# Moving the base product ahead in each turn, routing's side work off VectorE, and half-size last expert tiles

## The chip, the cores and the metric

One core of a Trainium2 chip runs the whole kernel. Its engines are TensorE (PE; its weight loads are listed as PEld), VectorE (DVE), ScalarE (ACT), GpSimd (POOL) and SyncE (SP, which only issues DMAs here). The metric is the device time of one execution in microseconds.

## The reference

The input x is 8 sequences of 512 rows of 128 numbers. After a layernorm (`xn`), the output is `x + attn(xn) + ffn(xn)`.

```python
def attn(x):                      # its x is xn; w is a vector of 127 biases by distance
    xn = (x - mean) / sqrt(var + EPS) * ln_w + ln_b
    u, v, base = split(silu(xn @ uv_w.T + uv_b), [256, 256, 128])
    q, k = rope(base * gamma[0] + beta[0]), rope(base * gamma[1] + beta[1])
    kernel = square(relu(q @ k.T / sqrt(128) + w[clipped distance]))
    return (u * (kernel @ v)) @ o_w.T + o_b + x

def ffn(x):                       # 4096 tokens, 8 experts, hidden width 512
    probs = sigmoid(x @ W_router); the two best of 8, weights p / (p1 + p2 + 1e-6)
    out = sq_relu(x @ W_sh_up) @ W_sh_down
    for e in the two experts: out += weight[e] * (sq_relu(x @ W_up[e]) @ W_down[e])
```

`rope` makes of the two halves x1, x2 of the 128 numbers `x1 cos - x2 sin` and `x2 cos + x1 sin`.

## The kernel before

The five engines run five programs written out by hand; they meet only at semaphores, and each engine works strictly in the order in which its program is written. Features lie on the 128 partitions, the 512 rows of a sequence along the columns.

**Turns.** A turn does one sequence: attention and the shared expert. Turns 0 to 6 come first, then the expert loop, then turn 7. `x1` is the once normalised sequence (for the shared expert and the router), `x2` the twice normalised one (for attention). Products that need precision are done as three matmuls in the type float32r on operands split in a high and a low part (`product`, lines L1021 to L1023, labelled `f32` in the profile's rows): ScalarE writes the high part, VectorE subtracts it from the operand for the low part. The others are plain f32 (`L1115` kernel times v, `L1101` shared down, `L1121` output, `L1284` expert down). A TensorE turn is, in order: the gates u0 and u1; two of the four shared up products sh0, sh1; the value products v0, v1 (12 matmuls of 256 columns); the scores qk0 to qk3, with the previous sequence's output product in their middle; sh2, sh3; two shared down products; the transposes `fin` of the previous sequence's output; kernel times v in four parts, between whose parts the next sequence is prepared (transposes of x2, the products `base` and `bsw`, transposes of x1); the last shared down products. `bsw` is the product for `base` with its two halves of features exchanged, so that the rotation needs no exchange. All of these go through a ring of four PSUM banks (`RING`): a product may start once the result four places before it has been read.

ScalarE turns `base` and `bsw` into two SiLU tiles and four scaled tiles `base_qk` (q and k, each plain and exchanged); VectorE multiplies by cos and sin (`rotate_base`) and adds (`rotate_sum`); ScalarE makes `qk_hi` from that, then the SiLU of u0 and u1, behind which the value products stand in the ring.

**Routing** is laid over turns 0 to 3. In turns 0 and 1 TensorE transposes each sequence's x1 once more (`rt`) and makes the router's products, eight columns each (`L1049`). At the end of turn 1 VectorE picks the two best experts of each token (`routing_first`, `routing_second`, semaphore `chosen_made`). In turn 2 TensorE counts (`routing_counted`), and VectorE makes the weights, running sums of the counts, each expert's number of tiles and the slot of each token (`routing_weights`, `routing_counts`, `routing_tiles`, `routing_slots`). With the slots (`slots_made`) GpSimd scatters the 4096 tokens in 64 indirect DMAs to `slots_in` in HBM, at most two in flight. In turn 3 VectorE makes the owners of the tiles (`routing_owners`); from it SyncE loads the expert weights.

**The expert loop** runs 39 tiles of 256 slots (`PAIR` = 2 halves of 128), enough for any distribution of the tokens. Step s transposes tile s, makes the up products of tile s - 1 (12 matmuls of 256 columns) and the down products of tile s - 2 (for each half four plain f32 matmuls of 128 columns); GpSimd sends the rows of tile s - 3 to `results`. Before the first step TensorE waits for `mixed` (turn 6's output added to x on VectorE) and for the slot load, which SyncE issues once all tokens have landed. The first 36 steps are in a loop unrolled by four, the rest is written out. Behind the last step VectorE does `rotate_base(7)`, TensorE turn 7; SyncE fetches the experts' rows (`fetch`) as soon as the last are home; VectorE adds them to x (`combine`), and SyncE stores.

## Time and profile before

| | us |
|---|---|
| three runs, median | 392.57 |
| their lowest and highest | 390.35, 453.52 |
| the profiled execution | 391.36 |
| its span | 389.5 |

| engine | busy, us | share of the span |
|---|---|---|
| TensorE | 351.0 | 90% |
| VectorE | 275.1 | 71% |
| ScalarE | 228.4 | 59% |
| GpSimd | 171.0 | 44% |

The span is what the trace shows from the first to the last record; the execution's own time is 1.9 us more. A busy share is a mean over stages with different limits, so the stages have to be looked at one by one. The mean granted clock of TensorE was 0.98 of full speed. In the timeline a row has the start, the busy time, engine, line, operation, `written<-read`, a count, and in brackets how long the engine stood idle before and what released it.

### The profile page before, as it was taken

What the parts mean: (1) busy time and instruction counts of PE and PEld (TensorE: products, weight loads), DVE (VectorE), ACT (ScalarE), POOL (GpSimd) and SP (SyncE); (2) the same over time, 40 slices, a digit from 0 to 9 for tenths busy, and PEclk for the clock granted to TensorE, in tenths of its full rate; (3) what the DMA queues carried; (4) which work ended last, traced back from release to release, by engine and by line L of the source; (5) the groups of instructions that cost most, each with busy time, mean ns of one, the idle gap of its engine ahead of it and who ended that gap; (6) DMA issues with size and microseconds to landing.
All of it is one profiled execution on the core that took longest, in us unless ns stands there. A gap on an engine that the chain in (4) does not pass through costs nothing.

```text
span 389.5 us, 6982 instructions
## 1 busy us (share of the span) xinstructions
PE 351.0 (90%) x1984; PEld 269.4 (69%) x1985; DVE 275.1 (71%) x646; ACT 228.4 (59%) x418; POOL 171.0 (44%) x161
## 2 busy tenths in 40 slices
PE   1779979989989999999996999999999999999791
PEld 1565658556556565756644989899899999998540
DVE  3879465789997774947643776777777777776876
ACT  0774996474653756646363767676676666772610
POOL 3004600000076377677760265666656566667000
PEclk9989999999999999999996999999999999999997
DMA  6999300000014811111112354544444446521795
GB/s 159 307 276 257 70 0 2 0 0 3 0 42 126 268 48 48 37 55 48 50 48 68 98 158 120 160 129 143 156 130 148 137 135 156 140 84 49 202 301 151
DMA packets 56836, 43.88 MB, mean 113 GB/s; under 512 B 6673, under 2 KB 49041, under 8 KB 56817
## 3 DMA queue, kind: packets, MB, share of 16 engines
q1 hardware_dynamic: 50304, 32.71, 32.6%
q0 software_dynamic: 4544, 9.38, 6.7%
q10 hardware_dynamic: 1968, 1.55, 1.3%
q8 instruction: 9, 0.15, 0.2%
q14 instruction: 11, 0.08, 0.1%
HBM read 26.36 MB, written 17.26 MB: 112 GB/s over the span
## 4 chain that ended last, share of the span: by engine, by line
PE 53%; DVE 16%; DMA 10%; ACT 10%; issue 6%; POOL 2%; ACTq 1%; DVEq 1%; SPq 0%
PE bank L1284 11%; DMA slot_x<-slots_in 9%; PE bank L1021 8%; PE bank L1115 8%; PE bank L1023 7%; PE bank L1022 7%; ACT base_qk L484 3%; PE bank L1101 3%; PE bank L1121 3%; PE bank L1261 2%; DVE work L762 2%; DVE work L756 2%; PE bank L1078 1%; ACT work L446 1%; ACT work L497 1%
## 5 line engine op out<-in xcount | busy, mean ns | idle before, releaser
L1008 POOL DMA_INDIRECT results<-work,dest x78 | 90.4, 1159 | 67.5 <-issue 22.4
L993 POOL DMA_INDIRECT slots_in<-work,slot_i x64 | 65.4, 1022 | 87.8 <-issue 62.6
L1284 PE MATMUL bank<-wdn,work 128*128 x624 | 76.1, 275 | 0.1
L1284 PEld LDWEIGHTS bank<-wdn,work 128*128 128x128 f32 x624 | 73.0, 192 | 0.3 <-issue 0.3
L1115 PE MATMUL bank<-kern,v 128*128 128x512 f32 x128 | 58.7, 592 | 0.0
L593 ACT ACTIVATE work<-bank 128x512 f32<-128x512 f32 x78 | 46.6, 600 | 6.5 <-PE bank L1023 3.9
L1021 PE MATMUL bank<-sx_lo,w_hi 128*128 128x256 f32 x156 | 48.3, 310 | 1.4 <-DVE w_lo L900 1.4
L1022 PE MATMUL bank<-sx_hi,w_lo 128*128 128x256 f32 x156 | 44.6, 286 | 0.0
L1023 PE MATMUL bank<-sx_hi,w_hi 128*128 128x256 f32 x156 | 44.5, 285 | 0.0
L584 ACT CAST sx_hi<-bank 128x256 fp32r<-128x256 f32 x39 | 14.5, 373 | 43.9 <-PE bank L1261 43.9
L906 DVE TENSOR_TENSOR work<-work 128x512 f32<-128x512 f32 x39 | 27.1, 694 | 18.7 <-ACT work L593 18.7
L1115 PEld LDWEIGHTS bank<-kern,v 128*128 128x128 f32 x128 | 22.7, 190 | 20.6 <-issue 20.6
L503 ACT ACTIVATE work<-bank 128x512 f32<-128x512 f32 x32 | 18.4, 600 | 27.0 <-PE bank L1101 26.0
L916 DVE TENSOR_SCALAR work<-bank,row_sum 128x128 f32<-128x128 f32 x78 | 27.2, 348 | 8.9 <-PE bank L1284 7.7
L1021 PEld LDWEIGHTS bank<-sx_lo,w_hi 128*128 128x128 f32 x156 | 30.1, 193 | 3.4 <-DVE sx_lo L897 1.8
L1022 PEld LDWEIGHTS bank<-sx_hi,w_lo 128*128 128x128 f32 x156 | 30.2, 194 | 0.0
L1101 PE MATMUL bank<-work,shdn 128*128 128x512 f32 x64 | 30.1, 593 | 0.0
L1023 PEld LDWEIGHTS bank<-sx_hi,w_hi 128*128 128x128 f32 x156 | 30.1, 193 | 0.0
L900 DVE TENSOR_TENSOR w_lo<-region,w_hi 128x512 fp32r<-128x512 f32 x39 | 26.8, 687 | 1.0
L586 ACT CAST w_hi<-region 128x512 fp32r<-128x512 f32 x39 | 24.3, 624 | 0.0
L597 ACT ACTIVATE work<-work 128x512 f32<-128x512 f32 x39 | 24.3, 622 | 0.0
L785 DVE SCALAR_TENSOR_TENSOR kern<-kern 128x512 f32<-128x512 f32 x32 | 22.2, 694 | 1.1
(163 smaller groups left out, 671.2 us busy)
## 6 DMA issues: line engine op xcount, KB each, us to landing
region<-in_L_ffn_W_up SPq DMA_DIRECT2D x39, 256.0 KB, 2.8
slots_in<-zeros SPq DMA_DIRECT2D x1, 5148.0 KB, 24.7
slot_x<-slots_in SPq DMA_DIRECT2D x39, 132.0 KB
region<-results SPq DMA_DIRECT2D x12, 256.0 KB, 5.0
wdn<-in_L_ffn_W_down SPq DMA_DIRECT2D x4, 512.0 KB, 6.3
out<-x_all SPq DMA_DIRECT2D x8, 256.0 KB, 2.3
results<-work,dest POOLq DMA_INDIRECT x78, 3.4
x_all<-in_L_attn_x SPq DMA_DIRECT2D x2, 512.0 KB, 7.6
```

The lines of the kernel that those rows point to most:

```text
L593: act.activation(hid_t[:, h, 2 * m:2 * m + 2, :].rearrange("p c s -> p (c s)"), P_UP[h][m][:, :], ACT.Relu)\
L900: dve.tensor_tensor(w_lo[:, j % 2, :], w_raw[:, j % 4, :], w_hi[:, j % 2, :].bitcast(F32), ALU.subtract).then_inc(w_lo_made, 1)
L906: dve.tensor_tensor(kept, kept, kept, ALU.mult).then_inc(hid_b_made, 1)
L916: dve.tensor_scalar(slot_y[:, k, :], P_Y[half][:, 0:D], times, None, ALU.mult).then_inc(y_made, 1)
L993: pool.indirect_dma_start(slots_in, bass.IndirectOffsetOnAxis(slot_i[:, k, t:t + 1], 0), xs1[:, t, at], None, element_offset=k * 2).then_i ...
L1008: pool.indirect_dma_start(results, bass.IndirectOffsetOnAxis(dest[:, at:at + 1], 0), slot_y[:, k, :], None).then_inc(returned[k], 16)
L1021: pe.matmul(dst, w_hi, m_lo, start=start, stop=False)
L1022: pe.matmul(dst, w_lo, m_hi, start=False, stop=False)
L1023: return pe.matmul(dst, w_hi, m_hi, start=False, stop=stop)
L1101: pe.matmul(P_OUT[:, :], shdn[:, c, :], sh[:, c % 2, :], start=(c == 0), stop=False).then_inc(shdn_done, 1)
L1115: last = pe.matmul(P_AV[e][:, :], v[:, j, e * P:(e + 1) * P], kern[:, j, :], start=(j == 0), stop=(j == TB - 1))
L1284: last = pe.matmul(P_Y[half][:, 0:D], hid_t[:, h, c, half * P:(half + 1) * P], wdn[:, of, c, :].rearrange("p a d -> p (a d)"), start=(c == ...
```

## The change

**Base chain.** The exchanged product `bsw` is gone. ScalarE makes one SiLU tile and two `base_qk` tiles. VectorE exchanges the halves as it multiplies by sin: two operations on 64 partitions each, which read one half and write the other. The next sequence's x2 transposes and base product move ahead of the shared down products and of kernel times v, and with them the work of ScalarE and VectorE on them. Sequence 7's rotation comes before the expert loop.

**x1.** The separate transposes of x1 are gone; the router's transposed copy is kept for all eight sequences (`route_xt`), and the split of x1 reads it.

**Routing.** The weights (sum, reciprocal, product) are GpSimd's; the copies of the counts and the second norm of sequences 2 and 3 are ScalarE's. The clearing of `sums` moves to turn 0. The split of x2 comes ahead of the routing steps.

**Tiles.** An expert's 128-slot halves are counted: its pairs go to full tiles, a last odd half to an own tile behind all full ones. There are still 39 tiles; the first 35 have 256 slots, the last four 128.

```diff
+FULL = (TOPK * NT + NE - 1) // PAIR
+SLOT_TILES = PAIR * FULL + TILES - FULL
...
-            RING += [("fin", b - 1)] if 0 < b < LAST else []
+            RING += [("x2", b + 1), ("fin", b - 1), ("base", b + 1)] if 0 < b < LAST else []
...
-            elif b < LAST:
-                RING += [("x2", b + 1), ("base", b + 1), ("bsw", b + 1), ("x1", b + 1)]
...
+                act.activation(silu_b[:, :], of_ring("base", b), ACT.Silu, bias=uvbias[:, 2:3]).then_inc(silu_b_made, 1)
+                act.wait_ge(silu_b_made, START + b + 1)
+                for k in range(2):
+                    act.activation(base_qk[:, k, :], silu_b[:, :], ACT.Identity, bias=bet[:, k:k + 1], scale=gam[:, k:k + 1])\
+                       .then_inc(base_made, 1)
...
+                if 0 < b < LAST:
+                    second_rows_hi(b + 1)
                 shared_relu(b, 2)
                 shared_relu(b, 3)
+                if 0 < b < LAST:
+                    base_silu(b + 1)
...
             def routing_tiles():
-                link(route_chain, dve.tensor_scalar(tiles_i[:, :], run[:, 15 + NT, :], float(PAIR * P - 1), None, ALU.add))
-                link(route_chain, dve.tensor_scalar(tiles_n[:, :], tiles_i[:, :], 8, None, ALU.logical_shift_right))
-                link(route_chain, dve.tensor_copy(ends[:, 0, 4:], tiles_n[:, :]))
-                for n in range(3):
+                pairs, odd = slice(0, NE), slice(NE, 2 * NE)
+                link(route_chain, dve.tensor_scalar(tiles_i[:, :], run[:, 15 + NT, :], float(P - 1), None, ALU.add))
+                link(route_chain, dve.tensor_scalar(tiles_i[:, :], tiles_i[:, :], 7, None, ALU.logical_shift_right))
+                link(route_chain, dve.tensor_scalar(parts_n[:, pairs], tiles_i[:, :], 1, None, ALU.logical_shift_right))
+                link(route_chain, dve.scalar_tensor_tensor(parts_n[:, odd], parts_n[:, pairs], -2.0, tiles_i[:, :], ALU.mult, ALU.add))
+                link(route_chain, dve.tensor_copy(ends[:, 0, 8:], parts_n[:, :]))
+                dve.tensor_scalar(in_pairs[:, :], ends[:, 0, 8:8 + NE], float(PAIR * P), None, ALU.mult)
+                for n in range(4):
...
             def routing_slots():
                 link(route_chain, dve.tensor_tensor(place, run[:, 15:15 + NT, :], place, ALU.add))
+                link(route_chain, dve.tensor_tensor(others, place, of_expert(in_pairs), ALU.is_ge))
+                link(route_chain, dve.tensor_tensor(others, others, of_expert(to_tail), ALU.mult))
+                link(route_chain, dve.tensor_tensor(place, place, of_expert(starts), ALU.add))
+                link(route_chain, dve.tensor_tensor(place, place, others, ALU.add))
...
+                for to, of in ((slice(0, HALF), slice(HALF, S)), (slice(HALF, S), slice(0, HALF))):
+                    dve.tensor_tensor(rot2[to], base_qk[of], cos_sin[of, 1:2, :].broadcast_to([HALF, 2, T]), ALU.mult)\
+                       .then_inc(rot2_made, 1)
...
+            pool.wait_ge(chosen_made, 1)
+            pool.tensor_tensor(denom[:, :], weight[:, 0, :], weight[:, 1, :], ALU.add).then_inc(weight_chain, 1)
...
+            pool.tensor_tensor(denom[:, :], denom[:, :], minus_one[:, :], ALU.pow).then_inc(weight_chain, 1)
...
+                    width = n.parts() * P
                     for c in range(HC):
-                        of = slice(c * P, (c + 1) * P)
-                        last = product(P_UP[h][c // 2][:, c % 2 * PAIR * P:(c % 2 + 1) * PAIR * P], w_hi[:, h, of], w_lo[:, h, of],
-                                       sx_hi[:, h, :], sx_lo[:, h, :])
+                        of, to = slice(c * P, (c + 1) * P), c % 2 * PAIR * P
+                        last = product(P_UP[h][c // 2][:, to:to + width], w_hi[:, h, of], w_lo[:, h, of],
+                                       sx_hi[:, h, 0:width], sx_lo[:, h, 0:width])
```

On VectorE in turn 2, before, the running sums (L716) stand ahead of the split of x2 (L671), the mix (L799, L802) and the tile counts (L722 on):

```order
L785 SCALAR_TENSOR_TENSOR kern<-kern 128x512
L712 COPY wdn<-bank 128x256
L713 COPY wdn<-bank 128x256
L716 TENSOR_TENSOR wdn<-wdn 128x256 x5
L671 TENSOR_TENSOR x_lo<-bank,x_hi 128x512
L799 TENSOR_TENSOR x_all<-x_all,work 128x512
L802 TENSOR_TENSOR x_all<-bank,x_all 128x512
L722 TENSOR_SCALAR tiles_i<-wdn 128x8
```

After, on VectorE, from the tile counts of turn 2 to the rotation (the split of x1 is L713, the slots L770 to L778, the exchange L799):

```order
L764 TENSOR_TENSOR to_tail<-to_tail,starts 128x8
L713 TENSOR_TENSOR x_lo<-region,x_hi 128x512
L770 TENSOR_TENSOR wdn<-wdn 128x256
L771 TENSOR_TENSOR wdn<-wdn,in_pairs 128x256
L772 TENSOR_TENSOR wdn<-wdn,to_tail 128x256
L773 TENSOR_TENSOR wdn<-wdn,starts 128x256
L774 TENSOR_TENSOR wdn<-wdn 128x256
L778 CAST slot_i<-slot_f 128x64
L796 TENSOR_TENSOR work<-base_qk,cos_sin 128x1024
L799 TENSOR_TENSOR work<-base_qk,cos_sin 64x1024 x2
```

The split of x2 now stands ahead of the sums, the split of x1 ahead of the slots, and the exchange takes two operations where one stood.

On TensorE in a middle turn, before, the next sequence's transposes (L1078) and base products stand between the parts of kernel times v (L1115), behind the shared down products (L1101) and `fin` (L1128):

```order
L1101 MATMUL bank<-work,shdn 128x512 x2
L1128 MATMUL bank<-cst,work 128x128 x4
L1115 MATMUL bank<-kern,v 128x512 x2
L1078 MATMUL bank<-cst,xs 128x128 x4
L1115 MATMUL bank<-kern,v 128x512 x2
...
L1078 MATMUL bank<-cst,work 128x128 x4
L1115 MATMUL bank<-kern,v 128x512 x4
L1101 MATMUL bank<-work,shdn 128x512 x2
```

After, at the same place (transposes L1134, shared down L1157, `fin` L1184, kernel times v L1171):

```order
L1134 MATMUL bank<-cst,xs 128x128 x4
L1157 MATMUL bank<-work,shdn 128x512 x2
L1184 MATMUL bank<-cst,work 128x128 x4
L1079 MATMUL bank<-x_lo,uvw_hi 128x512
L1080 MATMUL bank<-x_hi,uvw_lo 128x512
L1081 MATMUL bank<-x_hi,uvw_hi 128x512
L1171 MATMUL bank<-kern,v 128x512 x8
L1157 MATMUL bank<-work,shdn 128x512 x2
```

The transposes of x2 have moved ahead of the shared down products, one base product stands before kernel times v, and the transposes of x1 are gone.

## Rows read from the trace of the kernel before

**Rows 1.** Windows: busy of PE, PEld, DVE, ACT, POOL; granted clock; DMA.

```profile
24.80:26.90 2.10, 0.06 (x2) 0.05 (x1) 1.32 (x2) 1.56 (x3) 0.00 (x0) 1.00 1.24 276
26.90:30.30 3.40, 3.40 (x8) 2.75 (x9) 3.37 (x12) 2.27 (x4) 0.00 (x0) 0.50 1.26 253
141.50:165.00 23.50, 23.33 (x90) 14.52 (x89) 15.95 (x25) 13.71 (x22) 16.97 (x16) 1.00 0.15 47
328.70:357.10 28.40, 28.30 (x241) 27.42 (x239) 19.70 (x59) 17.92 (x35) 19.21 (x18) 1.00 0.36 103
```

**Rows 2.** Timeline: slot numbers, first scatter, first slot load, loop's start.

```profile
106.20 0.20 DVE L737 CAST slot_i<-slot_f 128x64 int32<-128x64 f32 x1
107.35 1.22 POOL L993 DMA_INDIRECT slots_in<-work,slot_i  x1 [57.75 <-issue]
204.34 7.50 SPq L364 DMA_DIRECT2D slot_x<-slots_in  x3
206.68 0.69 DVE L802 TENSOR_TENSOR x_all<-bank,x_all 128x512 f32<-128x512 f32 x1 [2.31 <-PE bank L1128]
208.28 1.11 PE L1261 MATMUL bank<-cst,slot_x 128*128 128x128 f32 x4 [1.65 <-DVE x_all L802]
```

**Rows 3.** Timeline: PE, the next sequence's base products and transposes, turn 4.

```profile
150.45 0.40 PE L1023 MATMUL bank<-x_hi,uvw_hi 128*128 128x512 f32 x1
150.69 0.60 PE L1078 MATMUL bank<-cst,work 128*128 128x128 f32 x4
151.13 3.60 PE L1115 MATMUL bank<-kern,v 128*128 128x512 f32 x8
```

**Rows 4.** Timeline: PE, first value product of turns 2 and 3.

```profile
86.56 0.39 PE L1021 MATMUL bank<-uvw_lo,x_hi 128*128 128x256 f32 x1 [1.39 <-ACT work L497]
112.36 0.39 PE L1021 MATMUL bank<-uvw_lo,x_hi 128*128 128x256 f32 x1 [1.39 <-ACT work L497]
```

**Rows 5.** Timeline: ACT, end of turn 0; PE, shared down products of turn 1.

```profile
45.25 1.26 ACT L479 ACTIVATE work<-bank,uvbias 128x512 f32<-128x512 f32 x2
46.40 1.52 ACT L484 ACTIVATE base_qk<-work,bet,gam 128x512 f32<-128x512 f32 x2
55.27 1.06 ACT L517 CAST qk_hi<-work 128x1024 fp32r<-128x1024 f32 x1
69.22 1.88 PE L1101 MATMUL bank<-work,shdn 128*128 128x512 f32 x4
```

**Rows 6.** Timeline: DVE, turns 1 and 2.

```profile
79.15 0.42 DVE L698 TENSOR_TENSOR wdn<-wdn 128x256 f32<-128x256 f32 x1
81.62 1.23 DVE L756 TENSOR_TENSOR work<-base_qk,cos_sin 128x1024 f32<-128x1024 f32 x1 [0.18 <-ACT base_qk L484]
97.73 2.26 DVE L716 TENSOR_TENSOR wdn<-wdn 128x256 f32<-128x256 f32 x5
100.03 0.69 DVE L671 TENSOR_TENSOR x_lo<-bank,x_hi 128x512 fp32r<-128x512 f32 x1
102.64 0.57 DVE L727 TENSOR_TENSOR ends<-ends 128x8 f32<-128x8 f32 x3
```

**Rows 7.** Timeline: PE, one expert tile (`x16`: two records a product).

```profile
276.21 0.28 PE L1023 MATMUL bank<-sx_hi,w_hi 128*128 128x256 f32 x1
276.33 1.95 PE L1284 MATMUL bank<-wdn,work 128*128 x16
278.11 0.38 PE L1261 MATMUL bank<-cst,slot_x 128*128 128x128 f32 x2
```

**Rows 8.** Chain of waits: 8-column products (two records each); a slot load.

```profile
65.72 0.79 PE bank L1049 x8
215.93 2.12 DMA slot_x<-slots_in
```

**Rows 9.** Timeline: start of the last turn.

```profile
357.58 0.50 PE L1021 MATMUL bank<-x_lo,uvw_hi 128*128 128x512 f32 x1 [0.45 <-DVE work L916]
362.84 0.38 PE L1021 MATMUL bank<-uvw_lo,x_hi 128*128 128x256 f32 x1 [2.24 <-ACT work L497]
```

312 lines of the change are left out of this document (166 added, 146 removed).

## The prediction

> **What bounds the kernel now.** I read the windows first, to see which engine is full where. In the middle turns TensorE works 23.33 of 23.50 us, and in the last stretch of the expert loop 28.30 of 28.40 [rows 1]; VectorE, ScalarE and GpSimd have room in both. So an edit pays in such a stretch only if it takes work off TensorE. The timeline then shows a second resource, which no share of busy time gives away: the scatter of the tokens. GpSimd issues 64 row scatters one behind the other, the first at 107.35, right after the slot numbers (106.20 + 0.20), and the first load of slots, which waits for all 64 to land, is issued at 204.34 [rows 2]. That is 97.9 us of pipeline, fixed by the first scatter. TensorE reaches the loop at 208.28, having waited for VectorE's last sum at 207.37 and then issued for 0.9 us [rows 2]. A slot load lands 2.1 us after its issue [rows 8], so data were there at about 206.5, and the scatter lies only some 2 us behind TensorE. What TensorE saves in the turns is worth no more than that, plus whatever the slot numbers move. The last stretch, from 357.58 on, is TensorE's turn 7 and then VectorE's sums; it begins with a wait of 2.24 us for the rotation [rows 9].
>
> **The turns.** Per sequence TensorE loses the product for `bsw` (three matmuls, 0.23 apart: 0.69 us) and the four transposes for `x1` (150.69 to 151.13: 0.44) [rows 3]: 1.13 us, of a turn of 23.5. The base product also moves from the middle of the value products to before them, so ScalarE and VectorE have 6.9 us more for the rotation; the short wait before the value products (23.50 - 23.33, and as much hidden in modelled ends) should go. I take 22.0 us a turn where nothing else binds. VectorE pays for it: the half swap is now two operations on 64 partitions instead of one on 128. Time on this engine goes with the columns of a partition (256 columns 0.42, 512 0.69, 1024 1.23 [rows 6]), so each half costs 1.23 and not 0.6, a pitch of 1.13 with the overlap: +1.13 a sequence, in cover except in turns 1 and 2, where routing fills VectorE.
> By the Trainium skill ("VectorE: DVE Perf Modes", Two Vector instructions with no wait between them) an operation whose input or output starts in another quadrant than the last one's is held until all earlier ones have finished. The trace has no such pair; by the rule each half would lose the overlap of about 0.1 us and the slot numbers below would come 0.2 to 0.3 us later. The sum below is made without it.
>
> **The slot numbers, step by step.**
> Turn 0 ends on ScalarE, which runs without a gap from 45.25 to 56.3. It loses one SiLU of two (half of 1.15) and two of the four `base_qk` (1.41) [rows 5], 2.0 us; the shorter start (no `x1` transposes, one product less) gives 0 to 0.5 more. I take 2.2: turn 1's shared up products, done at 69.2 before [rows 5], are done at 67.0.
> Turn 1: the transposes of x2 come right behind it (0.44), then ScalarE's copy and the split (0.6 + 0.7 [rows 6]) to 68.75; now `routing_first` (five operations of 0.46 pitch, 2.3) to 71.1, the mix of two 512-wide operations to 72.5, `routing_second` (seven of 0.46, 3.2) to 75.7. It ended at 79.57 before [rows 6], so chosen is 3.9 earlier. Then three rotation operations (3.4), `x1_lo` (0.6) and the sum (1.2): queries ready at 81.0; ScalarE's copy and SiLU, 1.9, and the first value product at 82.9 instead of 86.56 [rows 4]: 3.6 earlier.
> Turn 2: value products 1.44, counts 0.8, scores at 85.1; four scores, the output product and two shared products (5.9) bring TensorE to 91.0, with VectorE no longer in the way, since the routing weights, the second norm and two copies are gone from it. x2 split at 92.7, the counts' five additions (2.3 [rows 6]) to 95.0, the mix to 96.4. Then what the change adds: 13 linked operations of 0.2 (the three of 102.64 take 0.6 [rows 6]) and two unlinked, 2.85 instead of 1.4; the x1 split, 0.6; nine operations of 256 columns (five take 2.26 [rows 6]) where there were six, and the cast, 4.3. Slot numbers at 104.2 instead of 106.4: **2.2 us earlier**. The routing weights on GpSimd have from 75.7 to 104 to themselves: GpSimd idled 57.75 us before its first scatter [rows 2], so any price below some 28 us is hidden; ScalarE's copies and second norm lie in its idle time.
>
> **The price in turn 3.** Rotation comes behind the slot numbers: 104.2 + 3.4 + 1.2 = 108.8, then 1.9 on ScalarE: first value product of turn 3 at 110.9, before at 112.36 [rows 4]. TensorE will have been done with turn 3's shared up products at 105.7 (91.0, its remaining work of turn 2, 11.9, and 2.8), so it stands idle some 5 us. In the trace 2.1 idle us, from 24.8, were followed by 3.4 us at a granted clock of 0.50, the lower level of 1.2 GHz [rows 1]; the same again costs 1.7 us. TensorE's arrival: 110.9 + 1.7 + 3 turns of 22.0 = 178.6, plus the rest of turn 6 up to the loop (before from 112.36 + 3 x 23.5 = 182.9 to 208.28, 25.4; less 1.13) = 202.9. The scatter gives 204.34 - 2.2 + 2.2 = 204.4, which is later. So the loop starts at 204.4 instead of 208.28: **-3.9 us**, and of the 8 to 10 us that TensorE's own work shrinks half is lost waiting for the scatter.
>
> **The last turn.** Queries and keys of sequence 7 are ready before the loop. Today TensorE would reach the value products at 357.58 + 12 x 0.23 = 360.35 and starts them at 362.84 [rows 9]: **-2.5 us**. The next late thing is `fetch`, 16 loads behind the last returns; the returns come some 2 us sooner behind TensorE too, since the last tiles send one half each, so I leave it hidden; if not, it costs up to 1.
>
> **The tail tiles.** A full tile is two transposes (0.24), 12 products of the f32r type over 256 columns, 0.12 apart (1.43), and eight plain f32 products of 128 columns in 1.78, 0.22 each [rows 7]: 3.45. A half tile has one transpose (0.12), four such down products (0.89) and 12 up products over 128 columns, whose price no row shows. From below: half of 256 columns, 0.06 each. From above: the plain f32 product of the same 128 columns and the same four bytes, 0.22 [rows 7]. In between lies a floor by the weights: a product over only 8 columns still takes 0.10 a record [rows 8]. At 0.22 a half tile is 0.12 + 2.67 + 0.89 = 3.7 and four are 0.9 dearer than four full ones; TensorE's last waits in the loop (0.1 a tile) go under, so **+0.6 us** (0 to 0.9). At 0.10 a half tile is 2.2 and the four give 5.0; at 0.06 they would give 6.9, but VectorE still splits the whole 512 columns of weights for every tile, and I stop at 6. I take 0.22: the row with the same width and the same bytes, while 256 and 512 columns (0.12, 0.23) show only that the cheap rate holds from 256 up.
> By the Trainium skill ("TensorE: Matmul & The Clock Gate", LDWEIGHTS) a weight load takes columns / 1.2 ns, 107 ns for 128, and the 8-column rows at 0.10 agree. By that alone the up part is 12 x 0.107 = 1.28, and the time would be the first rival's.
>
> **Sum.** The profiled execution took 391.36: a span of 389.5 and 1.9 around it, and the runs shown have their median at 392.57, so the sum is 1.2 under what a median might show. 391.36 - 3.9 - 2.5 + 0.6 = 385.5, a gain of 1.5%. A measurement of this kernel tells about 2% from nothing.
>
> **Rivals.**
> A. Narrow products at the weight load's price or less (0.06 to 0.10). For it: the type ran at one column a clock at both widths shown. Against: no row under 256. 391.36 - 3.9 - 2.5 - 5.0 = 380.0, faster by 2.9%. Chance 0.34.
> B. The slot numbers come 2 us or more before 104.2, because VectorE overlaps its small operations or turn 0 shrinks by more. Then TensorE's arrival, 202.9, binds, and with tails as forecast the time is 384.0, 1.9% faster. For it: each step above was taken at its full pitch. Against: nine waits in a row, each only as early as its predecessor. Chance 0.10.
> C. The scatter slows down, and the kernel with it. Its pitch is 97.9 / 64 = 1.5 us; it now lies beside a denser TensorE and VectorE, and its rows share the DMA engines with the w_down and w_up loads. Each 0.1 us of pitch costs 6.4 us. From 1.6 the gain is gone, and at 1.7 it is 385.5 + 12.8 = 398.3, slower than before. Against: its pitch is steady across turns of very different load, and GpSimd touches none of the moved work. Chance 0.04.
> The forecast itself has 0.52.
>
> **How the numbers follow.** Own range of the forecast: 383.5 to 387.5 (slot numbers 1 us either way, `fetch` 1 us). Over all cases 378.8 to 388.0: the lower end takes in the tail's 5.0 and its 6, and C is left out. Faster by over 2% means under 383.5: all of A, a fifth of B and some of the forecast, 0.38; slower by over 2%, 0.03; within, 0.59.
>
> **What the next profile would show.** First scatter near 105.1 and slot load near 202; an idle time of about 5 us on TensorE before turn 3's value products with the clock at 0.50 behind it; middle turns of 22.0; TensorE waiting for the slot load, not for VectorE, at the loop's start; in the tail up products 0.22 apart; no wait of 2.24 in the last turn. I am wrong if the up products are 0.10 or less apart, or if the slot numbers do not move by 1 to 3 us.

## The result, and the profile after

The changed kernel takes 390.2 us (median of 20 runs, 387.0 to 395.1), the kernel before 392.95 (20 runs). The ratio, taken like all ratios below from the fast runs of both kernels, is 0.993 [0.990, 0.995] (in brackets its 95% interval): a gain of 0.7%, no difference at 2%. Forecast was 385.5, the range ended at 388.0. The profiled execution took 395.13, a span of 393.3, which is 4.9 over its median, so its stages are checked below against the traces of other kernels that share them.

**Turns, timeline and windows** (columns as in [rows 1]). First the slot numbers, the first scatter, the issue of the first slot loads, turn 6's last sum and the loop's first transposes:

```profile
106.07 0.20 DVE L778 CAST slot_i<-slot_f 128x64 int32<-128x64 f32 x1
107.33 1.23 POOL L1051 DMA_INDIRECT slots_in<-work,slot_i  x1 [19.79 <-issue]
206.79 0.90 SPq L374 DMA_DIRECT2D slot_x<-slots_in  x2
204.42 0.69 DVE L845 TENSOR_TENSOR x_all<-bank,x_all 128x512 f32<-128x512 f32 x1 [1.12 <-PE bank L1184]
209.10 0.69 PE L1313 MATMUL bank<-cst,slot_x 128*128 128x128 f32 x2 [4.71 <-DMA slot_x<-slots_in]
```

Against [rows 2] the slot numbers moved by 0.1 us and not by 2.2, so the scatter did not move either; TensorE was ready earlier and waited 4.71 us. A middle turn, the stretch behind turn 3's wait, the body of the expert loop, and the last tiles:

```profile
141.50:163.50 22.00, 22.00 (x83) 13.78 (x82) 17.27 (x26) 12.15 (x20) 16.51 (x16) 1.00 0.15 49
110.00:118.00 8.00, 4.80 (x17) 4.38 (x18) 5.50 (x7) 5.03 (x9) 6.36 (x6) 0.63 0.13 42
215.00:325.00 110.00, 105.32 (x862) 100.69 (x861) 78.90 (x231) 73.37 (x147) 64.18 (x55) 0.99 0.47 136
352.60:366.00 13.40, 12.30 (x58) 11.27 (x59) 3.28 (x10) 3.92 (x10) 3.83 (x4) 0.62 0.06 24
```

A middle turn is full at 22 us. The body of the loop is not: 862 records of TensorE in 110 us, and the same stretch of the kernel before had 884 (below). The stretch with the last tiles ran at a mean granted clock of 0.62.

TensorE in turns 2 and 3 (first value product, then two value products and one product of the scores), and VectorE at the end of turn 2, against [rows 4] and [rows 6]:

```profile
84.71 0.39 PE L1079 MATMUL bank<-uvw_lo,x_hi 128*128 128x256 f32 x1 [1.36 <-ACT work L520]
113.20 0.58 PE L1079 MATMUL bank<-uvw_lo,x_hi 128*128 128x256 f32 x1 [5.42 <-ACT work L520]
113.58 0.41 PE L1080 MATMUL bank<-uvw_hi,x_lo 128*128 128x256 f32 x1
113.79 0.41 PE L1081 MATMUL bank<-uvw_hi,x_hi 128*128 128x256 f32 x1
116.35 0.63 PE L1080 MATMUL bank<-qk_hi,qk_lo 128*128 128x512 f32 x1
```
```profile
98.53 0.16 DVE L750 TENSOR_SCALAR tiles_i<-wdn 128x8 int32<-128x8 f32 x1
101.34 0.69 DVE L713 TENSOR_TENSOR x_lo<-region,x_hi 128x512 fp32r<-128x512 f32 x1
...
106.18 1.22 DVE L796 TENSOR_TENSOR work<-base_qk,cos_sin 128x1024 f32<-128x1024 f32 x1
107.43 2.47 DVE L799 TENSOR_TENSOR work<-base_qk,cos_sin 64x1024 f32<-64x1024 f32 x2
110.00 1.23 DVE L805 TENSOR_TENSOR work<-work 128x1024 f32<-128x1024 f32 x1
```

In turn 3 products stand 0.21 us apart where 0.12 is usual: the engine had idled 5.42 us. The half-partition operations take 1.24 each with no overlap.

**The tail, timeline of TensorE.** L1313 are transposes (of tiles 33, 34, 35 and 38, counted from 0; half tiles from 342.14 on), L1337 down products, the others up products:

```profile
332.95 0.38 PE L1313 MATMUL bank<-cst,slot_x 128*128 128x128 f32 x2
338.65 0.44 PE L1313 MATMUL bank<-cst,slot_x 128*128 128x128 f32 x2 [2.10 <-DMA slot_x<-slots_in]
342.14 0.27 PE L1313 MATMUL bank<-cst,slot_x 128*128 128x128 f32 x1
348.86 0.28 PE L1080 MATMUL bank<-sx_hi,w_lo 128*128 128x128 f32 x1
348.98 0.27 PE L1081 MATMUL bank<-sx_hi,w_hi 128*128 128x128 f32 x1
349.09 0.28 PE L1079 MATMUL bank<-sx_lo,w_hi 128*128 128x128 f32 x1
352.62 0.33 PE L1313 MATMUL bank<-cst,slot_x 128*128 128x128 f32 x1 [1.42 <-DMA slot_x<-slots_in]
356.18 0.41 PE L1079 MATMUL bank<-sx_lo,w_hi 128*128 128x128 f32 x1
356.39 0.41 PE L1080 MATMUL bank<-sx_hi,w_lo 128*128 128x128 f32 x1
363.26 0.80 PE L1079 MATMUL bank<-x_lo,uvw_hi 128*128 128x512 f32 x1 [0.44 <-DVE work L961]
366.72 0.28 PE L1079 MATMUL bank<-uvw_lo,x_hi 128*128 128x256 f32 x1
```

Narrow up products are 0.11 apart. But two waits for slot loads stand here, and behind the second one the products are 0.21 apart: the granted clock was 0.50, the lower level of 1.2 GHz, from 354.3 to 364.6. In the last turn the value products (366.72) follow without the wait of [rows 9].

**One step of the loop** shows what those waits are. Timeline of VectorE, SyncE and TensorE, transposes of tiles 21 and 22 (L961 weights the down products' result, L974 makes the destinations, L374 is the slot load):

```profile
288.07 0.38 PE L1313 MATMUL bank<-cst,slot_x 128*128 128x128 f32 x2
288.27 0.35 DVE L961 TENSOR_SCALAR work<-bank,row_sum 128x128 f32<-128x128 f32 x1 [0.20 <-PE bank L1337]
289.21 0.23 DVE L974 TENSOR_TENSOR dest<-row_sum,spare_row 128x2 int32<-128x2 f32 x1 [0.21 <-DVE spare_row L971]
289.62 0.37 SPq L374 DMA_DIRECT2D slot_x<-slots_in  x1
292.11 0.44 PE L1313 MATMUL bank<-cst,slot_x 128*128 128x128 f32 x2 [0.44 <-DMA slot_x<-slots_in]
```

There are two slot buffers. With s = 20 in these rows: the load for tile s + 2 waits until VectorE has taken the destinations of tile s out of the buffer, and VectorE does that last in its step, behind the two weightings of tile s - 2 (`step` on VectorE). So it is issued 1.5 us after the transposes of tile s + 1 have begun, and 2.5 us after its issue TensorE begins to transpose what it brought, 4.04 us behind the last transposes. For a tile TensorE needs 3.45 us, so it waits.

A table by stages, all from the transposes' and first gate products' starts in the traces (start of the loop; to tile 3; from there to tile 35 and per tile; to turn 7's u0; to the end of the span). The kernels are those of the experiments below. The traces of after and full_same are of executions 4.9 and 3.8 us over the kernel's median; the others are within 1.6 of theirs.

| kernel | loop starts | to tile 3 | 32 tiles (each) | rest of loop | last turn |
|---|---|---|---|---|---|
| before | 208.28 | 9.8 | 119.5 (3.73) | 20.0 | 31.9 |
| after | 209.10 | 10.4 | 122.6 (3.83) | 21.1 | 30.0 |
| full_same | 207.83 | 11.3 | 121.3 (3.79) | 23.8 | 29.4 |
| full_short | 205.13 | 10.9 | 119.1 (3.72) | 20.0 | 29.5 |
| flight4 | 206.09 | 10.1 | 122.0 (3.81) | 17.5 | 29.5 |
| before_slots4_e | 209.58 | 8.8 | 111.1 (3.47) | 20.8 | 33.4 |
| slots4 | 207.75 | 9.2 | 110.5 (3.45) | 16.2 | 29.4 |
| slots4_full_e | 206.35 | 9.8 | 110.5 (3.45) | 19.7 | 29.4 |
| best | 202.79 | 9.5 | 110.5 (3.45) | 16.2 | 29.5 |

### The profile page after: what moved, and what is told of

Same layout as the page of the kernel before. It is cut to its first block, busy times and chain, and to the rows that moved or that the text cites. A ratio compares the mean times of both kernels' runs of the same rounds, so it can differ in the third digit from the quotient of the medians.

```text
span 393.3 us, 6680 instructions
## 1 busy us (share of the span) xinstructions
PE 345.5 (88%) x1891; PEld 266.7 (68%) x1892; DVE 282.8 (72%) x647; ACT 214.9 (55%) x404; POOL 179.2 (46%) x164
## 4 chain that ended last, share of the span: by engine, by line
PE 34%; DMA 31%; DVE 15%; issue 7%; ACT 6%; POOL 5%; DVEq 0%; SPq 0%; POOLq 0%; ACTq 0%
DMA slots_in<-work,slot_i 19%; PE bank L1337 11%; DMA slot_x<-slots_in 11%; PE bank L1079 6%; PE bank L1081 5%; PE bank L1080 5%; POOL slots_in L1051 3%; PE bank L1313 2%; ACT work L456 2%; PE bank L1171 2%; POOL inv L990 1%; DVE work L799 1%; DMA x_all<-in_L_attn_x 1%; PE bank L1134 1%; DVE wdn L667 1%
## 5 line engine op out<-in xcount | busy, mean ns | idle before, releaser
L1337 PE MATMUL bank<-wdn,work 128*128 x592 | 75.3, 281 | 0.6 <-DVE work L961 0.6
L1337 PEld LDWEIGHTS bank<-wdn,work 128*128 128x128 f32 x592 | 71.8, 197 | 0.9 <-issue 0.9
L1171 PE MATMUL bank<-kern,v 128*128 128x512 f32 x128 | 56.7, 592 | 0.0
L1079 PE MATMUL bank<-sx_lo,w_hi 128*128 128x256 f32 (+1 forms) x156 | 49.0, 314 | 1.4 <-DVE w_lo L945 1.4
L631 ACT ACTIVATE work<-bank 128x512 f32<-128x512 f32 (+1 forms) x78 | 45.0, 577 | 9.4 <-PE bank L1081 6.7
L1081 PE MATMUL bank<-sx_hi,w_hi 128*128 128x256 f32 (+1 forms) x156 | 45.5, 292 | 0.0
L1080 PE MATMUL bank<-sx_hi,w_lo 128*128 128x256 f32 (+1 forms) x156 | 45.4, 291 | 0.0
L1171 PEld LDWEIGHTS bank<-kern,v 128*128 128x128 f32 x128 | 24.1, 190 | 26.8 <-issue 26.3
L620 ACT CAST sx_hi<-bank 128x256 fp32r<-128x256 f32 (+1 forms) x39 | 14.1, 362 | 50.5 <-PE bank L1313 50.5
L951 DVE TENSOR_TENSOR work<-work 128x512 f32<-128x512 f32 (+1 forms) x39 | 25.9, 665 | 19.0 <-ACT work L631 18.8
L961 DVE TENSOR_SCALAR work<-bank,row_sum 128x128 f32<-128x128 f32 x74 | 25.8, 348 | 11.7 <-PE bank L1337 11.5
L1157 PE MATMUL bank<-work,shdn 128*128 128x512 f32 x64 | 30.2, 594 | 0.0
L1313 PE MATMUL bank<-cst,slot_x 128*128 128x128 f32 x74 | 16.2, 301 | 13.0 <-DMA slot_x<-slots_in 12.8
L540 ACT CAST qk_hi<-work 128x1024 fp32r<-128x1024 f32 x8 | 8.4, 1046 | 33.9 <-DVE work L805 33.9
L526 ACT ACTIVATE work<-bank 128x512 f32<-128x512 f32 x32 | 18.8, 598 | 12.5 <-PE bank L1157 11.1
L825 DVE SCALAR_TENSOR_TENSOR kern<-bank,bias_t 128x512 f32<-128x512 f32 x32 | 21.9, 685 | 4.2 <-PE bank L1081 4.2
```

The costliest lines, as they stand in the source:

```text
L631: act.activation(hid_t[:, h, 2 * m:2 * m + 2, 0:width], made, ACT.Relu).then_inc(relu_done, 1)
L951: dve.tensor_tensor(kept, kept, kept, ALU.mult).then_inc(hid_b_made, 1)
L961: dve.tensor_scalar(slot_y[:, k, :], P_Y[half][:, 0:D], times, None, ALU.mult).then_inc(y_made, 1)
L1079: pe.matmul(dst, w_hi, m_lo, start=start, stop=False)
L1080: pe.matmul(dst, w_lo, m_hi, start=False, stop=False)
L1081: return pe.matmul(dst, w_hi, m_hi, start=False, stop=stop)
```

## The experiments

Two theories stood at first: S, that the scatter binds the loop's start, so that what the turns save is lost there, and T, that in the tail a slot load's round trip is longer than a half tile. After experiment 2 a third took T's place: L, that this round trip paces the whole loop. Ratios are to the kernel before.

**1. Four scatters in flight (flight4): 387.19 us, 0.986 [0.981, 0.992].**

```diff
-        IN_FLIGHT = TOPK
+        IN_FLIGHT = 2 * TOPK
```

> The changed kernel with four scatters of tokens in flight instead of two; nothing else differs. In its trace the 64 scatters take 97 us, of which GpSimd's own issues are 69.2 and waits for landed rows 23.7, and TensorE waits 4.71 us for the first slot load before the loop and then works 6 us at the lower clock. Theory S (the scatter binds the loop's start, so what the turns save is lost there): the pitch falls from 1.52 to 1.3 or less, the load of slots is issued at 190 or before, the wait of 4.71 goes, the loop starts at about 205.5 (behind turn 6's last sum) instead of 209.1 with a shorter stretch at the lower clock: 384 to 386.5 us, a ratio of 0.978 to 0.984 against the kernel before. Rival (GpSimd's issues set the pitch, not the landings): pitch 1.45 or more and the time stays at 390, ratio 0.993.

The loop starts behind turn 6's sum, not behind the load:

```profile
198.27 11.12 SPq L374 DMA_DIRECT2D slot_x<-slots_in  x3
```
```profile
206.09 0.65 PE L1313 MATMUL bank<-cst,slot_x 128*128 128x128 f32 x4 [1.65 <-DVE x_all L845]
```

The load is issued 8.5 us earlier, a pitch of (198.27 - 107.42) / 64 = 1.42 and not the 1.3 expected: GpSimd's own issues fill 69 of these 91 us. TensorE's arrival, 206.1, takes over after 3.0 us. So the scatter did bind the loop's start in the changed kernel, but removing that gave only 3.0 us (0.7%; the two intervals still touch), and the time missed the expected 386.5: the loop remained 149.7 us long.

**2. Four slot buffers (slots4): 375.28 us, 0.957 [0.953, 0.961].**

```diff
-        slot_x = sb("slot_x", [P, 2, 2, ROW_W])
+        slot_x = sb("slot_x", [P, 4, 2, ROW_W])
...
-                    sp.wait_ge(sx_turned, i * UNROLL + (j + 1))
                     sp.wait_ge(dest_made, i * (PAIR * UNROLL) + PAIR * (j + 1))
-                    load_slots(j, ds(i * (PAIR * UNROLL) + PAIR * (j + 2), PAIR))
+                    load_slots(j, ds(i * (PAIR * UNROLL) + PAIR * (j + 4), PAIR))
```

> The changed kernel with four buffers for the loaded slots instead of two, so a tile's load may be issued four steps ahead (SyncE no longer waits for the transposes by name; the destinations come behind them). Theory T (in the tail the round trip of a slot load, transposes, destination, load of 2.8 us, over two short steps is longer than the steps; TensorE waits 1.42 and 0.64 us and falls to the lower clock for 9 us; another wait of 2.10 hits a full tile): waits for slot loads go from the whole loop but for its start, the tail's four tiles run 0.11 us a product at the higher clock, 3.5 to 5.5 us less: ratio 0.980 to 0.985. Rival (the waits are those of the loads' own queue, which is busy, or of VectorE): the waits stay at other loads, and the ratio is 0.99 or more.

Both theories fell short: the gain is not 3.5 to 5.5 us but 15. The round trip paced every tile, not the tail alone. Body of the loop, then TensorE's waits for slot loads from the loop's start to turn 7 (total, times, longest), first of this kernel:

```profile
215.00:325.00 110.00, 110.00 (x958) 109.60 (x958) 85.61 (x257) 79.84 (x161) 72.44 (x62) 1.00 0.50 151
```
```profile
PE bank L1312 <- DMA slot_x<-slots_in: 3.6, 2, 3.4
```

and of the changed kernel with two buffers:

```profile
PE bank L1313 <- DMA slot_x<-slots_in: 12.8, 16, 4.7
```

In 110 us TensorE now has 958 records instead of 862. The waits listed fell by 9.2 us, the loop by 154.2 - 135.8 = 18.4, and against flight4's trace, which is not of a long execution, by 13.8. The modelled ends of the matmuls cover a part of each wait: in the changed kernel the transposes stand by turns some 3.6 and 3.9 to 4.0 us apart, the list has 0.2 to 0.4 of the longer step and nothing of the shorter, and the distance from one tile's transposes to the next tells it whole.

**3. The tail undone (full_same: 391.77 us, 0.995 [0.991, 0.998]) and with it its routing (full_short: 387.74, 0.988 [0.984, 0.993]).** In the first, whose edit is shown, all 39 tiles are full but the long routing stays; in the second `routing_tiles`, `routing_slots` and `routing_owners` are those of the kernel before.

```diff
-FULL = (TOPK * NT + NE - 1) // PAIR
+FULL = TILES
...
-                link(route_chain, dve.tensor_scalar(tiles_i[:, :], run[:, 15 + NT, :], float(P - 1), None, ALU.add))
-                link(route_chain, dve.tensor_scalar(tiles_i[:, :], tiles_i[:, :], 7, None, ALU.logical_shift_right))
-                link(route_chain, dve.tensor_scalar(parts_n[:, pairs], tiles_i[:, :], 1, None, ALU.logical_shift_right))
-                link(route_chain, dve.scalar_tensor_tensor(parts_n[:, odd], parts_n[:, pairs], -2.0, tiles_i[:, :], ALU.mult, ALU.add))
+                link(route_chain, dve.tensor_scalar(tiles_i[:, :], run[:, 15 + NT, :], float(PAIR * P - 1), None, ALU.add))
+                link(route_chain, dve.tensor_scalar(tiles_i[:, :], tiles_i[:, :], 8, None, ALU.logical_shift_right))
+                link(route_chain, dve.tensor_scalar(parts_n[:, pairs], tiles_i[:, :], 0, None, ALU.logical_shift_right))
+                link(route_chain, dve.scalar_tensor_tensor(parts_n[:, odd], parts_n[:, pairs], -1.0, tiles_i[:, :], ALU.mult, ALU.add))
```

> The changed kernel with 39 full tiles: the tail is undone, while routing keeps its added operations (an expert's odd half gets a full tile; the factor for odd halves is zero). Theory T (the tail's cheaper products are eaten by slot load waits and the lower clock): within 1 us of the changed kernel, ratio 0.990 to 0.998. Rival N (narrow products at 0.11 us really give 4 x 1.1 us, and the loss is only upstream, at the scatter and the clock): 3.5 to 4.5 us slower than the changed kernel, ratio 1.001 to 1.005.

> The changed kernel with the tail undone and the routing of tiles, slots and owners as in the kernel before: only the turns and routing's side work are changed. Against the run with 39 full tiles and the long routing it shows what the added operations on VectorE cost: the slot numbers should come 1.4 + 1.3 = 2.8 us before 106.3, and by theory S the whole scatter, the first slot load and the loop start 2.8 us earlier too, so 2.5 to 3 us less than that run (ratio lower by 0.007). Rival (TensorE binds the loop's start, the scatter does not): less than 1 us between the two.

Half tiles gave 0.2% in the changed kernel (0.993 against 0.995, whose intervals overlap), as theory T said, and not rival N's 1%. The long routing cost 0.6% by the ratios, 2.5 us (4.0 by the medians), though these intervals too overlap; the start of the loop moved by 2.7 (207.83 to 205.13), close to the 3.0 us by which the slot numbers moved (106.04 to 102.99):

```profile
102.99 0.20 DVE L765 CAST slot_i<-slot_f 128x64 int32<-128x64 f32 x1
104.25 1.23 POOL L1036 DMA_INDIRECT slots_in<-work,slot_i  x1 [17.48 <-issue]
```
```profile
205.13 1.23 PE L1298 MATMUL bank<-cst,slot_x 128*128 128x128 f32 x4 [4.82 <-DMA slot_x<-slots_in]
```

So the tail part of the change as a whole lost, by 0.993 with it to 0.988 without (390.2 and 387.7 us); the two intervals, [0.990, 0.995] and [0.984, 0.993], overlap, so the time alone does not prove it, while the 3 us at the slot numbers and at the loop's start are in the traces.

**4. Was the kernel before paced too (before_slots4)?** The edit of experiment 2 in the kernel before.

> The kernel before with four buffers for the loaded slots instead of two; nothing of the change. Theory L (the slot load's round trip, not TensorE, paces the expert loop in the kernel before too: its transposes stand 3.74 us apart over 38 tiles, where the run with four buffers has 3.44): the loop falls from 149.3 to about 138.5, so 381 to 383 us, ratio 0.970 to 0.975, and the change is then worth 6 to 8 us between the two kernels with four buffers. Rival (TensorE paces the loop before, as its busy share of the last stretch said; only the changed kernel's loop suffers): ratio 0.99 or more.

This experiment was one of ten (before_slots4, slots4_full, slots4_flight4 and slots4_filler, each once more as _b, and before_slots4_c and slots4_full_c) that fell on three chips (6, 8 and 15 in the record) on which the kernel before itself took 441 to 443 us by its median: in the turns, while the scatter ran, ScalarE and VectorE stood still for 10 to 40 us at a time, as in this row of ScalarE in slots4_flight4:

```profile
197.30 1.26 ACT L519 ACTIVATE work<-bank,uvbias 128x512 f32<-128x512 f32 x2 [39.38 <-remote]
```

Its repeats:

> The kernel before with four slot buffers once more, since on the chip of the first try engines stood still for 10 to 40 us in the turns, in every kernel. In that trace the transposes of the loop already stood 3.44 us apart where nothing else was late. Theory L: ratio 0.970 to 0.975. Rival (TensorE paced the loop before): 0.99 or more.

> One look at the kernel before with four slot buffers. Theory L: the loop's transposes 3.44 to 3.5 us apart instead of 3.74, loop from first transposes to the last turn's first product 138 to 140 us instead of 149.3, and a time of 381 to 383 where the kernel before takes 392.5. Rival (TensorE paced the loop before): 3.7 apart, 389 or more.

The first gave 436.7 us, a ratio of 0.992 [0.987, 0.998], which is the rival's number; the others took 439.6 beside 442.5, and 445.9 beside 440.9. With halts of this length in the turns I take nothing from these times (there the kernel with four scatters in flight was 20 us behind its neighbours, which no theory here explains). A single run on a chip without the halts (before_slots4_d) took 384.06 beside 392.97, with the transposes 3.43 to 3.6 apart:

> One look at the kernel before with four slot buffers, on another occasion. Theory L: loop from first transposes to the last turn's first product 138 to 140 us instead of 149.3, 381 to 383 where the kernel before takes 392.5. Rival: transposes 3.7 apart, 389 or more.

And six runs there:

> The kernel before with four slot buffers, timed in rounds (the look at it took 384.06 where the kernel before took 392.97). Theory L: ratio 0.973 to 0.980. The change is then worth, between the two kernels with four buffers, 0.9568 over that ratio, 1.7 to 2.4%. Rival (the look was a lucky one): 0.985 or more.

Measured: 384.24 us, 0.978 [0.974, 0.982], as theory L said. The body of the loop, of the kernel before and with four buffers:

```profile
215.00:325.00 110.00, 106.03 (x884) 101.83 (x883) 80.94 (x238) 74.40 (x149) 66.02 (x57) 1.00 0.48 139
```
```profile
215.00:325.00 110.00, 110.00 (x951) 109.10 (x950) 85.15 (x254) 80.30 (x162) 70.65 (x61) 1.00 0.49 149
```

The kernel before was paced by the slot load, at 3.73 us a tile where TensorE needs 3.47. With four buffers in both, the change is worth 0.957 / 0.978 = 0.978, 9 us. By the table, of the 10.6 us between the two spans the loop's start has 1.8, the rest of the loop 4.6 and the last turn 4.0. Not all of that is half tiles and rotation: this run's turn 7 begins behind a wait of 1.53 us, where the kernel before waited 0.45, and its value products, behind the same wait for the rotation as before (2.23), ran at a granted clock of 0.50 from 355.4 to 358.8, where the kernel before ran at full rate; that is 1.1 and about 1.5 us.

**5. Half tiles once loads do not pace (slots4_full_e).** Experiments 2 and 3 (first) together.

> The changed kernel with four slot buffers and with 39 full tiles, routing's added operations kept: what the half tiles are worth once loads do not pace the loop. Theory L: TensorE sets the tail's pace, a half tile costs 12 x 0.11 + 8 x 0.11 + 0.12 = 2.3 to 2.4 us instead of 3.44, so the run is 4 to 4.5 us slower than the one with four buffers and half tiles: 379.5, ratio 0.966 to 0.969. Rival (the tail stays bound by VectorE, ScalarE or the weights' loads, so half tiles give little): within 1.5 us of it, ratio under 0.961.

> The changed kernel with four slot buffers and 39 full tiles, once more. Theory L: half tiles are worth 4 to 4.5 us there, ratio 0.966 to 0.969. Rival: within 1.5 us of the run with half tiles, under 0.961.

> One look at the changed kernel with four slot buffers and 39 full tiles. Theory L: 379 to 380.5, 4 to 4.5 us over the 375.3 with half tiles. Rival: under 377.

Those three fell on the same chips (424.1, 418.1 and 427.9 us) and are left aside too; ahead of six runs on a chip without the halts:

> The changed kernel with four slot buffers and 39 full tiles, timed in rounds. Theory L: half tiles are worth 4 to 4.5 us there, ratio 0.966 to 0.969. Rival (the tail is bound by VectorE or ScalarE): under 0.961.

Measured: 377.08 us, 0.960 [0.956, 0.964], only 1.8 us over the run with half tiles, so by the time the rival's number came out. The stages say otherwise: from tile 35 on the loop is 3.5 us longer with full tiles and from its start 4.1 (139.96 against 135.82), as theory L had it, but this run's loop began 1.4 us earlier (from the first scatter to the first slot load the traces with two in flight have 96.3 to 99.5 us). Of the size, 1.8 to 4.1 us for four tiles, no more can be said. Half tiles lose some 0.9 us of their own: each of them writes the same bank, so the last one's down products wait 0.64 us for VectorE, and turn 7 behind them waits 0.72, where it waits 0.44 behind full tiles; VectorE's last weighting, at 343.17, had itself waited 1.72 us for rows to be sent home:

```profile
341.70 1.15 PE L1336 MATMUL bank<-wdn,work 128*128 x8 [0.64 <-DVE work L960]
343.57 0.50 PE L1078 MATMUL bank<-x_lo,uvw_hi 128*128 128x512 f32 x1 [0.72 <-DVE work L960]
```

**6. The lower clock of turn 3 (slots4_filler).** Four slot buffers, and matmuls whose result is not used, in turn 3 between the shared up products and the value products.

```diff
+                if route == 3:
+                    pe.wait_ge(counts_copied, 2)
+                    for _ in range(11):
+                        pe.matmul(P_ROUTE[:, :], shdn[:, 0, :], bias_t[:, 0:T], start=True, stop=True)
```

> The changed kernel with four slot buffers, and eleven matmuls into an unused bank (their result is not used; 0.45 us each) in TensorE's wait of 5.4 us in turn 3. The clock theory (a wait of some us lowers the granted clock, and the 6.8 us behind it run at half speed and cost 2.9 us): turn 3's value products and scores run at 0.12 and 0.23 us a product, not at 0.21 and 0.43, and TensorE comes to the loop 2.5 to 3 us earlier. By theory S, with two scatters in flight, this does not show in the time, since the first slot load stays where it is: TensorE waits 5.5 to 6.5 us before the loop instead of 3.35, and the ratio stays at 0.955 to 0.959. Rival (the end of the turns binds, the scatter does not): 2 to 3 us faster, ratio 0.949 to 0.952.

> The changed kernel with four slot buffers and eleven matmuls into an unused bank in turn 3's wait, once more. Clock theory with theory S: turn 3's products at full rate, TensorE 2.5 to 3 us earlier at the loop, where it waits longer for the slot load, the ratio at 0.955 to 0.959. Rival: ratio 0.949 to 0.952.

Both fell on the chips with the halts (420.7 and 423.2 us beside 442.8 and 442.5), so their times say nothing; turn 3 lies ahead of the halts and can be read. I had priced these matmuls at 0.45 (each has two records of that), they took 0.82, 9.0 us in all:

```profile
106.57 9.60 PE L1224 MATMUL bank<-bias_t,shdn 128*128 128x512 f32 x22
115.60 0.68 PE L1078 MATMUL bank<-uvw_lo,x_hi 128*128 128x256 f32 x1
116.12 0.28 PE L1079 MATMUL bank<-uvw_hi,x_lo 128*128 128x256 f32 x1
...
120.13 0.79 PE L1078 MATMUL bank<-qk_lo,qk_hi 128*128 128x512 f32 x1
```

The value products began 2.4 us later than in the changed kernel (115.60 against 113.20), yet the third scores came only 0.16 later (120.13 against 119.97); the granted clock was 1.00 here from 113 to 121, and 0.50 there from 112.0 to 118.8. Full rate gave back 2.2 us. That is the price of the lower clock behind this wait.

**7. Four buffers, four scatters in flight, six such matmuls (best): 370.13 us, 0.943 [0.939, 0.947].** Four buffers and four in flight alone were run only on the chips with the halts (443.3 and 442.6 us beside 442.8 and 442.5, the ratio of the first 1.006 [0.999, 1.012]).

> The changed kernel with four slot buffers and four scatters in flight. Theory S (the scatter binds the loop's start by 3.35 us in the run with four buffers): the slot load is issued at 198.3, the loop starts at 206 behind turn 6's sum with a shorter wait ahead of it, and less of it at the lower clock: 1.5 to 4 us less than 375.3, ratio 0.947 to 0.953. Rival (the start of the loop is given back, as everything in the loop waits for something else): within 1 us of 375.3, ratio 0.955 to 0.959.

> The changed kernel with four slot buffers and four scatters in flight, once more. Theory S: ratio 0.947 to 0.953. Rival: 0.955 to 0.959.

And of the version with all three:

> The changed kernel with four slot buffers, four scatters in flight, and six matmuls into an unused bank (result not used, 0.90 us each) in turn 3's wait. Theory S with the clock theory: the first slot load at 198.5; turn 3's value products and scores at full rate, which brings TensorE to the loop about 2.3 us earlier; loop start at 204 to 204.5 instead of 207.75: 371 to 372.5 us, ratio 0.944 to 0.949. Rival (what is won at the loop's start is given back in the loop): 0.954 or more.

```profile
202.79 0.72 PE L1316 MATMUL bank<-cst,slot_x 128*128 128x128 f32 x4 [1.65 <-DVE x_all L844]
```

The loop starts at 202.79, 5.0 us before that of slots4, all of which shows in the time (375.28 to 370.13): with the pacing gone, nothing behind the loop's start gives it back. It is 0.9 us under the expected range; turn 1 was not hit by the lower clock here (below), and the slot numbers came at 105.33. How much of the 5.0 us four scatters in flight give and how much the six matmuls (the value products of turn 3 start at 112.46, the wait of 5.42 is 0.28, and the clock stays at full speed) was not separated on a chip without the halts. This version beats both kernels, by 5.7 and 5.1%.

## Why the prediction was wrong

**The bound (the reading that hid the loop's pace).** I wrote that TensorE works 28.30 of 28.40 us in the loop and that "an edit pays in such a stretch only if it takes work off TensorE". That stretch [rows 1] is the loop's last, where tiles follow at 3.5 to 3.6 us. Over its body TensorE was busy 106.03 of 110, and 32 tiles took 3.73 each while my own price of a tile was 3.45: 39 tiles at that price are 134.6 us, the loop took 149.3. I did not divide. Of these 14.7 us four buffers gave back 8.7 in the kernel before (149.3 to 140.6). Experiments 2 and 4 show that the slot load's round trip set the pace, before and after. It did not spoil the sum of differences as such, since both kernels have it; it decides what a cheaper tile can give.

**Loop start, -3.9, from "Slot numbers at 104.2 instead of 106.4: 2.2 us earlier": this is the step of the sum that failed.** It came out at +0.8 in the profiled run; over the four traces with the same turns, routing and two in flight (after, full_same, slots4, slots4_full_e: 209.10, 207.83, 207.75, 206.35) the mean is 207.8, -0.5. That the scatter sets it was right (experiments 1 and 3), and so was its length within 1 us or so. Wrong was the slot numbers' 104.2; they came at 106.3, no earlier than before. The late parts of the chain:
- Turn 1's shared up products were to be done at 67.0 and were at 68.5. ScalarE did come out of turn 0 2.2 us earlier (the queries' high part at 53.04 instead of 55.27 [rows 5]), but two waits of 0.6 and 0.3 us ahead of the value products were followed by a granted clock of 0.50 from 57.4 to 60.8 and products 0.21 apart: the twelve value products took 2.7 us and not 1.5. Nothing in the sum had this. Here of the changed kernel, then of full_short, where the same waits were followed by full rate:

```profile
54.81 0.63 PE L1134 MATMUL bank<-cst,work 128*128 128x128 f32 x4 [0.61 <-ACT work L520]
55.76 1.06 PE L1105 MATMUL bank<-wr,region 128*128 128x8 f32 x8 [0.33 <-ACT region L465]
58.57 0.41 PE L1080 MATMUL bank<-uvw_hi,x_lo 128*128 128x256 f32 x1
```
```profile
55.57 0.63 PE L1119 MATMUL bank<-cst,work 128*128 128x128 f32 x4 [0.63 <-ACT work L521]
56.52 1.06 PE L1090 MATMUL bank<-wr,region 128*128 128x8 f32 x8 [0.32 <-ACT region L466]
58.78 0.28 PE L1065 MATMUL bank<-uvw_hi,x_lo 128*128 128x256 f32 x1
```

- In full_short and best, whose turn 1 ran at full rate, the shared up products end at 67.8, since turn 0 gave only 1.5 us there, and the first value product of turn 2 starts at 83.9 to 84.0; in the others at 84.7 to 85.0. I forecast 82.9. So 1.5 of the 1.8 us missed there had come by the end of turn 1, and some 1.1 of these 1.5 is the lower clock. The other 0.3 is about what the rotation adds, next.
- Each rotation took 3.8 us to the start of the sum and not 3.4. The three operations do not overlap. This is what the Trainium skill says ("VectorE: DVE Perf Modes", Two Vector instructions with no wait between them): an instruction whose operands start in another group of 32 partitions is held until all earlier ones have finished. I had set it aside, and the trace agrees, with 0.4 where I had worked out 0.2 to 0.3 from the rule.
- What was added to VectorE was sized right: tiles 2.8 (2.85 forecast), slots 4.3 (4.3).

**Middle turns, 22.0: right** (21.95 and 21.90 from one value product to the next). **Turn 3's wait, about 5 with the lower clock behind it: right** (5.42); the clock cost 2.2 and not 1.7. (The terms of the forecast, 108.8 and 1.9, add up to 110.7 and not 110.9.) TensorE's arrival at the loop was 206.1 (flight4) and not 202.9, by the 2.3 us that v0(3) was late and the 0.5 of clock, and 0.4 more.

**Tail, +0.6: the term rested on the wrong row.** I took 0.22 a narrow product from the plain f32 row of the same width; it is 0.11, close to rival A's 0.10. By the Trainium skill ("TensorE: Matmul & The Clock Gate", LDWEIGHTS) a weight load takes columns / 1.2 ns, so an estimate of 107 ns for 128 columns, and the trace agrees with 0.11. But rival A's time, 380.0, did not come either: TensorE's saving, up to 4.1 us (experiment 5), met the pace of the slot loads, which a shorter step does not quicken. In flight4's trace, with a wait of 1.10 us ahead of tile 38 and a clock of 1.00 behind it, 2.5 us of it were left in the rest of the loop; in the profiled run nothing (21.1 us against 20.0 before), since behind the wait of 1.42 the clock fell.

**The loop's body, not in my sum: +1.8 to 3.2 us over 32 tiles.** 3.79 to 3.83 a tile in after, full_same and flight4, 3.73 and 3.72 in before and full_short. One slot load of 4.5 us (334.18 to 338.65) is 2.1 of it in the profiled run, one of 4.1 is 1.7 in flight4's. The rest, 0.8 to 1.8, goes with the destinations' operation, which in the kernels with the long routing starts 0.11 us later once in four tiles (1.14 behind the transposes instead of 1.03), with the load behind it 0.17 later than in the kernel before (1.55 and 1.38), always at the same place of the loop, and never in the other two; in a loop paced by exactly this chain that counts. That it is the cause was not tested, and why it is late there stays open.

**Last turn, -2.5: right.** From u0 to the end 29.4 to 30.0 us instead of 31.9, and the wait is gone.

**Sum.** The forecast was 4.7 us too low (385.5 for 390.2). The loop's start has 3.4 of it (207.8 for 204.4). Another 1.6 is the base: I counted from the one execution of 391.36, and the kernel before has its median at 392.95. The loop and the last turn behind its start come to about nothing together: in flight4's trace the tail is 3.1 quicker than forecast, the 32 tiles 2.6 and the first three 0.3 slower. That they nearly cancel is luck. The range ended too early because all its cases but C took the slot numbers' 2.2 us for granted within 1, and none had the loop paced by a load. Rival C, the scatter's pitch, did not come: from the first scatter to the first slot load's issue it is 99.5 us in the profiled run against 97.0 in the kernel before (the 97.9 of the prediction counts from the slot numbers [rows 2]), and 96.3 to 98.6 in the other four traces of the changed turns with two in flight. (GpSimd did take over routing's weights, though the prediction says that it touches none of the moved work; it was done with them 19.79 us before its first scatter.)

## What to carry to other kernels

Multiply your price of one iteration by their number and hold it against the loop's length before calling an engine its bound; a busy share of 96% with many short waits can be a chain of another engine and a DMA that paces every step. A buffer is free only when its last reader is done, so look where in that reader's step the read stands: here 2 KB a partition for two more buffers were worth 8 us in the kernel before, more than the rebuilt base chain with routing's side work (full_short, 4.6 us). Whether two buffers would do if VectorE read the destinations ahead of its weightings was not tried. When one stage waits for a long pipeline, what the stage before it saves is worth nothing until that pipeline moves, and the waits it leaves can cost clock as well.

## What the runs showed of the hardware

- Products of the type float32r over 128 columns are 0.11 us apart (after, 348.86 to 349.09), over 256 0.12, over 512 0.23 [rows 7 and 3]: from 256 to 128 columns next to nothing is saved.
- Three multiplications of 1024 columns, one on 128 and two on 64 partitions that read one half and write the other, have a pitch of 1.25 (after, 106.18, 107.43) and not the 1.13 of those on 128 partitions in the kernel before (106.31, 107.44, 108.57).
- Behind waits of no more than 0.6 and 0.3 us, close together, the granted clock of TensorE was 0.50 for 3.4 us in five traces of the changed kernels (after, full_same, flight4, slots4, slots4_full_e), and 1.00 in two with the same waits (full_short, best). Behind the wait of 5.4 us in turn 3 it was 0.50 for 6.8 us in all five traces that have it, at a price of 2.2 us. Behind one of 2.2 us in the last turn it was 1.00 in the kernel before and 0.50 for 3.4 us in both readable traces of that kernel with four buffers.
- A slot load of 132 KB lands 2.1 to 2.6 us after its issue in slots4; in three of the four traces of changed kernels with two buffers one load took 4.1 to 4.5 (after, flight4, full_same), and TensorE waited 1.7 to 2.1 us for it. With four buffers the longest, 3.4 (slots4_full_e), left no such wait.
